# A graph layer with routed experts: longer VectorE instructions in the edge sort, and four places for finished output tiles

## The reference

```python
def reference(x, src, dst, edge_weight, ...):      # x: 12500 x 256; 212500 edges, sorted by their second list
    # graph layer
    h = layernorm(x) @ W                            # 256 x 256
    msgs = h[dst] * edge_weight[:, None]            # edge_col = dst
    x = x + segment_sum(msgs, src, 12500) + bias    # edge_row = src
    # experts: E = 8, top K = 2, D = 256, H = 512
    xn = layernorm(layernorm(x)) * gamma + beta
    logits = xn @ Wr + br
    w = softmax of the two largest logits, zero for the other experts
    for e in range(8):
        y += w[:, e] * (gelu(xn @ W1[e] + b1[e]) @ W2[e] + b2[e])
    return x + y
```

## Time and profile before

| | us |
|---|---|
| median of 3 runs | 4042.66 (4030.87 to 4053.49) |
| the profiled execution | 4048.99 |
| its span, first to last instruction | 4047.2 |
| TensorE busy | 3080.1 |
| POOL busy | 2636.6 |
| VectorE busy | 2538.3 |
| ScalarE busy | 1084.7 |

### The profile page before, as it was taken

How to read it: one execution, slowest core, us unless ns; L and a number is a source line. 1 busy time by engine, 2 the same in 40 slices (tenths; PEclk the granted TensorE clock), 3 DMA queues, 4 the chain that set the end, 5 groups by cost and what they waited for, 6 DMA issues and landing times.

```text
span 4047.2 us, 74660 instructions
## 1 busy us (share of the span) xinstructions
PE 3080.1 (76%) x20376; PEld 2068.7 (51%) x20376; DVE 2538.3 (63%) x6473; ACT 1084.7 (27%) x2341; POOL 2636.6 (65%) x2487
## 2 busy tenths in 40 slices
PE   7677434322698989989899898888998989099973
PEld 4445334321355555555555555555555556088762
DVE  8699658532466666666666666666666665145553
ACT  1353110000122222222222223222222222066542
POOL 1241778887777777777777777777777776620354
PEclk9899766655799999999999999999999999599987
DMA  5331110002344443434344434334344346552453
GB/s 156 108 110 58 36 29 13 7 10 59 111 114 116 116 117 110 117 112 117 110 114 113 115 111 118 113 110 113 112 112 120 109 116 102 174 165 86 131 179 113
DMA packets 288422, 420.11 MB, mean 104 GB/s; under 512 B 89734, under 2 KB 218315, under 8 KB 288139
## 3 DMA queue, kind: packets, MB, share of 16 engines
q0 software_dynamic: 109280, 279.33, 25.1%
q1 hardware_dynamic: 112536, 72.81, 6.4%
q10 hardware_dynamic: 66324, 64.42, 4.9%
HBM read 339.36 MB, written 76.98 MB: 103 GB/s over the span
## 4 chain that ended last, share of the span: by engine, by line
PE 35%; DVE 16%; issue 10%; POOL 6%; DVEq 5%; DMA 4%; SPq 1%; ACTq 0%; ACT 0%; POOLq 0%
PE bank L1775 13%; PE bank L1705 6%; PE bank L1758 4%; POOL area L749 4%; DVE area L1296 3%; PE bank L1707 3%; PE bank L1843 3%; PE bank L1860 2%; DVEq L1311 2%; DVE area L1304 2%; POOL zs L766 1%; DMA out_dram<-area 1%; DVE rel L1293 1%; DVEq L1304 1%; DVE rq L1341 1%
## 5 line engine op out<-in xcount | busy, mean ns | idle before, releaser
L749 POOL DMA_INDIRECT area<-h_table,listed x1856 | 1862.6, 1004 | 612.3 <-issue 545.6
L1705 PE MATMUL bank<-area 128*128 x2608 | 881.0, 386 | 75.4 <-issue 38.0
L1707 PE MATMUL bank<-area 128*128 x2608 | 718.8, 276 | 0.0
L899 ACT ACTIVATE area<-bank,b_t 128x512 f32<-128x512 f32 x384 | 263.8, 687 | 1454.1 <-PE bank L1758 902.5
L1775 PE MATMUL bank<-w2h,area 128*128 128x256 f16 x3072 | 591.3, 295 | 0.0
L1304 DVE TENSOR_TENSOR area<-area,listed 128x1024 f16 x652 | 423.0, 690 | 107.6 <-DVE area L1296 91.1
L1705 PEld LDWEIGHTS bank<-area 128*128 x2608 | 257.1, 99 | 412.4 <-issue 181.9
L717 POOL DMA_INDIRECT edge_list<-area,didx x256 | 414.8, 1620 | 77.2 <-issue 77.2
L1758 PE MATMUL bank<-area,w1h 128*128 128x512 f16 x1536 | 458.8, 381 | 0.0
L1775 PE MATMUL bank<-w2l,area 128*128 128x256 f16 x1536 | 453.8, 295 | 0.0
L1429 DVE SCALAR_TENSOR_TENSOR area<-bank,wfull,area 128x256 f32<-128x256 f32 x384 | 168.3, 480 | 302.1 <-PE bank L1775 302.1
(11 more groups left out here) (289 smaller groups left out, 4977.6 us busy)
## 6 DMA issues: line engine op xcount, KB each, us to landing
area<-h_table,listed POOLq DMA_INDIRECT x1856
area<-in_x_dram SPq DMA_DIRECT2D x194, 128.0 KB, 2.2
area<-zs SPq DMA_DIRECT2D x66, 256.0 KB, 2.8
ys<-area ACTq DMA_DIRECT2D x66, 256.0 KB
out_dram<-area ACTq DMA_DIRECT2D x100, 128.0 KB, 2.7
h_table<-area SPq DMA_DIRECT2D x97, 128.0 KB, 1.7
xt<-in_x_dram ACTq DMA_DIRECT2D x97, 128.0 KB
area<-in_L_ffn_W_dram ACTq DMA_DIRECT2D x16, 512.0 KB, 3.9
```

Of the source, the lines that this page charges most:

```text
L749: pool.indirect_dma_start(out=stage[:, (k % RU) * UNIT + 2 * D * c:(k % RU) * UNIT + 2 * D * (c + 1)], out_offset=None, in_=h_table[:, :], ...
L899: nc.scalar.activation(h32[:, m, :], psH[m][:, :], ACT.Gelu, scale=1.0 / WSCALE, bias=b1_t[:, e * KH + m:e * KH + m + 1])
L1705: nc.tensor.matmul(psA[:, :], target[:, ds(at, P, 2)], stage[:, ds(rows, 2 * D)], start=False, stop=False)
L1707: last = nc.tensor.matmul(psA[:, 0:D], target[:, ds(at + TGT // 2, P, 2)], stage[:, ds(rows, D)], start=False, stop=False)
```

## The change

Four edits:

- The output places `ot` and their semaphores `s_ofin` go from two to four (`RX`), so a combine waits for the store of the tile four before, not two before.
- The first four PSUM banks become two tensors of two banks (`twin`). One `copy_predicated` takes two banks; `s_kept` counts pairs of banks, and TensorE waits by pairs.
- `field` is stored in pairs of columns, `[CH // 2, NF, 2]`, so that one VectorE product takes all four fields of a group. The two values of a column pair stay adjacent.
- In `records` the two record parts are written for the four groups of a batch at once.

```diff
-        ot = blk(fp32, 2, D)
+        ot = blk(fp32, RX, D)
-        field = sort(fp16, NF, CH)
+        field = sort(fp16, CH // 2, NF, 2)
...
-        bank = [ctx.enter_context(nc.psum_tensor(f"bank{i}", [P, 512], fp32)) for i in range(8)]
+        twin = [ctx.enter_context(nc.psum_tensor(f"twin{i}", [P, 2, 512], fp32)) for i in range(2)]
+        bank = [twin[i // 2][:, i % 2, :] for i in range(4)]
+        bank += [ctx.enter_context(nc.psum_tensor(f"bank{i}", [P, 512], fp32)) for i in range(4, 8)]
...
-            nc.gpsimd.tensor_tensor(field[:, 3, :], wgt[:, :], field[:, 2, :], ALU.subtract).then_inc(s_wfield, 1)
+            nc.gpsimd.tensor_tensor(field[:, :, 3, :], by_two(wgt), field[:, :, 2, :], ALU.subtract).then_inc(s_wfield, 1)
...
-                for k in range(NBK):
-                    dve.wait_ge(s_place, NBK * i + k + 1)
-                    nc.vector.copy_predicated(posp[:, cols[k]], maskp[:, i % 2, cols[k]],
-                                              ps_pos[k][:, 0:BC]).then_inc(s_kept, 1)
+                for w in range(2):
+                    dve.wait_ge(s_place, NBK * i + 2 * w + 2)
+                    nc.vector.copy_predicated(by_bank(posp, w), by_bank(maskp[:, i % 2, :], w),
+                                              twin[w][:, :, 0:BC]).then_inc(s_kept, 1)
...
-                for f in range(NF):
-                    two = field[:, f, c].rearrange("p (j e) -> p j e", e=2).unsqueeze(2)
-                    ins = nc.vector.tensor_tensor(
-                        rhs[:, h, :, f, :, :], eqq[:, h, :, :, :], two.to_broadcast([P, GC // 2, Q, 2]), ALU.mult)
-                ins.then_inc(s_build, 1)
+                pairs = slice(g * GC // 2, (g + 1) * GC // 2)
+                nc.vector.tensor_tensor(
+                    rhs[:, h, :, :, :, :], eqq[:, h, :, :, :].unsqueeze(2).to_broadcast([P, GC // 2, NF, Q, 2]),
+                    field[:, pairs, :, :].unsqueeze(3).to_broadcast([P, GC // 2, NF, Q, 2]),
+                    ALU.mult).then_inc(s_build, 1)
...
-                for j in range(BATCH):
-                    nc.vector.tensor_tensor(
-                        rec[:, j, :, 0:RUN].bitcast(i32), got[:, j, 0, :].rearrange("p (r k) -> p r k", r=RQ),
-                        low3[:, j, :].rearrange("p (r k) -> p r k", r=RQ), ALU.add)
+                nc.vector.tensor_tensor(
+                    rec[:, :, :, 0:RUN].bitcast(i32), got[:, :, 0, :].rearrange("p j (r k) -> p j r k", r=RQ),
+                    low3[:, :, :].rearrange("p j (r k) -> p j r k", r=RQ), ALU.add)
...
-                if j >= 2:
-                    dve.wait_ge(s_ofin[j % 2], 16 * (j // 2))
+                if j >= RX:
+                    dve.wait_ge(s_ofin[j % RX], 16 * (j // RX))
...
-                        pe.wait_ge(s_kept, NBK * (i - 1) + k + 1)
+                        pe.wait_ge(s_kept, 2 * (i - 1) + k // 2 + 1)
```

More of the change, by code:

```diff
@@ L222, in gnn_moe_layer_kernel, with by_two @@
         area = sb("area", [P, AREA // 4], fp32)
+        def by_two(a):
+            return a.rearrange("p (j e) -> p j e", e=2)
         class Carve:
@@ L493, in gnn_moe_layer_kernel @@
         s_o = sem("s_o")
-        s_ofin = [sem("s_ofin0"), sem("s_ofin1")]
+        s_ofin = [sem(f"s_ofin{i}") for i in range(RX)]
         def reached(eng, s, value, gate=True):
@@ L790, in _ @@
             nc.scalar.activation(half_h[:, :], bkt_b[:, :], ACT.Copy).then_inc(s_cast, 1)
-            nc.scalar.activation(field[:, 2, :], wgt[:, :], ACT.Copy).then_inc(s_cast, 1)
+            nc.scalar.activation(field[:, :, 2, :], by_two(wgt), ACT.Copy).then_inc(s_cast, 1)
             act.wait_ge(s_prep, 7)
-            nc.scalar.activation(field[:, 1, :], src_i[:, :], ACT.Copy).then_inc(s_cast, 1)
+            nc.scalar.activation(field[:, :, 1, :], by_two(src_i), ACT.Copy).then_inc(s_cast, 1)
             act.wait_ge(s_prep, 8)
-            nc.scalar.activation(field[:, 0, :], dst_i[:, :], ACT.Copy).then_inc(s_cast, 1)
+            nc.scalar.activation(field[:, :, 0, :], by_two(dst_i), ACT.Copy).then_inc(s_cast, 1)
             def norm(t):
@@ L982, in store_out @@
                 act.wait_ge(s_o, j + 1)
-                act.dma_start(out_rows(routed[j]), ot[:, j % 2, :]).then_inc(s_ofin[j % 2], 16)
+                act.dma_start(out_rows(routed[j]), ot[:, j % RX, :]).then_inc(s_ofin[j % RX], 16)
             turned(0)
@@ L1000, in _ @@
             act.wait_ge(s_ost, 16 * (NSET + 1))
-            for k in range(2):
-                act.wait_ge(s_ofin[k], 16 * len(range(k, NR, 2)))
+            for k in range(RX):
+                act.wait_ge(s_ofin[k], 16 * len(range(k, NR, RX)))
         @block.vector
@@ L1119, in pair_masks @@
                     dve.wait_ge(s_place, NBK * (i - 1))
-                    dve.wait_ge(s_kept, NBK * (i - 1))
+                    dve.wait_ge(s_kept, 2 * (i - 1))
                 if i == 0:
@@ L1135, in tab, with by_bank @@
                 dve.wait_ge(s_tab, tabs[0])
+            def by_bank(a, w):
+                return a[:, 2 * w * BC:2 * (w + 1) * BC].rearrange("p (k c) -> p k c", k=2)
             cols = [slice(k * BC, (k + 1) * BC) for k in range(NBK)]
@@ L1218, in _ @@
                     places()
-            dve.wait_ge(s_kept, NBK * (NT // 2))
+            dve.wait_ge(s_kept, 2 * (NT // 2))
             nc.vector.tensor_scalar(sh_f[:, :], bucket_h[:, :], 12.0, None, ALU.mult)
@@ L1271, in records @@
                 post(nc.vector.tensor_scalar(low3[:, :, :], bint[:, :, :], 7, None, ALU.bitwise_and))
[L1272 to L1279 removed]
+                nc.vector.tensor_tensor(
+                    rec[:, :, :, 0:RUN].bitcast(i32), got[:, :, 0, :].rearrange("p j (r k) -> p j r k", r=RQ),
+                    low3[:, :, :].rearrange("p j (r k) -> p j r k", r=RQ), ALU.add)
+                nc.vector.tensor_tensor(
+                    rec[:, :, :, RUN:2 * RUN], rown[:, :, :].rearrange("p j (r k) -> p j r k", r=RQ),
+                    dest[:, :, :, 2].unsqueeze(3).to_broadcast([P, BATCH, RQ, RUN]), ALU.add).then_inc(s_posted, 1)
             for g in range(NGRP):
@@ L1677, in _ @@
                     pe.wait_ge(s_tables, 1)
-                    pe.wait_ge(s_kept, NBK * (NT // 2))
+                    pe.wait_ge(s_kept, 2 * (NT // 2))
                 if j == 0 and B >= 2:
```

8 lines of the change are left out of this document (2 added, 6 removed).

## The result

The changed kernel takes 4013.05 us at the median of 6 runs (4006.43 to 4019.76) against 4043.48 of the kernel before (6 runs, the three from before the change among them). The ratio is 0.9921, 95% interval 0.9907 to 0.9936: 30 us faster, where 3993 was forecast, inside the range of 3970 to 4022. The profiled execution took 4012.82 us (span 4010.7), 36.5 us less in the span than that of before.

A forecast was written before the change was run, and what follows sets the result against it. Limits taken: VectorE in the place loop, POOL in the sort, output-store waits in the tail. 32 + (10 + 1.2 + 0.4) + 6 = 50 us off 4048.99 gave 3999, or 3993 us for the median; range 3970 to 4022.

The forecast's parts named there:

- The tail's waits for stores: Expert blocks that also combine tiles: four places remove the combine's wait for store landing; 17 blocks, 32 us less (23 to 41).
- POOL becomes the limit or nearly: Tail: with the store waits gone, POOL's two tile fetches per block, 6.2 to 7.3 us, set or nearly set the pace.
- the 6.7 us: Tail: block pace taken for 15 of the 17 blocks, from POOL's two fetches; the first two blocks at 6.4 us.
- Products: Sort: one product of 3328 elements saves 0.20 us per group; 10 us through scatters plus 1.2 us before the first.
- The argument by held scatters: Sort: POOL gets through once per group; a held scatter's 3.30 us wait shrinks by 0.20, 6% of 167 us, 10 us.
- Records: Sort: two record instructions for eight save 0.4 us per batch; only the first batch counts, 0.4 us (0 to 6).
- Copies: Place loop: two-bank copies take 1.99 us instead of 2.12 per iteration; 48 iterations, 6 us less (0 to 17).
- The estimate of 0.25 us per iteration: Place loop: the skill's 120 cycles plus one per element for a PSUM source; two copies fewer save 12 us in all.
- The halved rate: Rival, 0.05: the sort's long product loses its doubled rate and scatters wait longer; 49 us slower, 4092 us.
- The gathers did not take the stores' place: Rival, 0.13: in the tail VectorE holds POOL's gathers, a block takes 8 us; 27 us gained in all, 4015 us.
- nor did TensorE's pace come: Rival, 0.14: the tail runs at TensorE's pace and the copies save twice as much; 65 us gained, 3978 us.
- The signs: Marks of being right: tail pace 6.4 to 6.9 us, product 1.9, long scatters 4.1, place iteration 3.6, second tail part unchanged.

## Why the prediction was right and where not

- **The tail's waits for stores.** Right in the mechanism: the landing is gone from the chain. The term was mis-sized, 32 us forecast and 15.7 measured (17 to 22 with the places alone). The step that failed is "two stores in each such block, 0.99 us together ..., which I let cost 0.25 us of the block". That issue lies in a ring through ScalarE and VectorE in which nothing is idle, so it costs all of its 1.05 us, and the read of the expert's number behind it takes 0.59 us in place of 0.28. The pace is 6.15 + 1.05 + 0.31 and 0.1 between them, 7.6 us; a block of 6.4 us was never near. I had taken 6.14 us as TensorE's pace with slack on ScalarE. The rows for the right sum stood in the trace of before, where the same stretch was 2.48 us. Why the read takes longer behind the stores stays open.
- **"POOL becomes the limit or nearly."** Wrong for this change, where POOL waited for combines 11 times, up to 1.7 us; right once the ring was shortened, at 6.33 us, which is two fetches at the quick end of my 6.2 to 7.3. That fetch time came true, and the 6.7 us did not matter.
- **Products.** Rate as forecast (1.88 us). The gain passed through POOL: 9 to 13 us alone where 11.2 were forecast. The argument by held scatters gave nearly the right size, but the runs show a simpler path: the scatters that end beside VectorE's work are fixed in number, so the whole saving, 4 x 0.2 us per batch, comes off.
- **Records.** 0.4 us forecast, 4 to 7 measured alone; my upper end was 6. That the other fifteen batches "lie inside POOL's time" was the wrong picture.
- **Copies.** 6 us forecast, and the place loop is 6.3 us shorter, but only 2 of it are the copies': 0.07 us per iteration, not 0.13. A copy of 832 elements takes 1.079 us, so 416 elements more cost 0.467 us where I had taken 0.44; of the step of 0.50 us between copies that leaves about 0.03 us as what a second copy costs for itself, and not 0.06. The estimate of 0.25 us per iteration, from the Trainium skill, VectorE: DVE Perf Modes, section on the TRN2 errata, is further off. The rest is POOL's meetings with VectorE, which the forecast did not have: the size of this term came out right by luck.
- **The rivals.** The halved rate did not come (1.88 us against the 2.8 from which it decides). Its price has a slip: 3.57 less 2.10 us is 1.47 and not 1.55, by which the same sum gives 45 us slower and not 49. The gathers did not take the stores' place in the changed kernel (no combine of the 17 blocks waits for them), though the measured 4013 us lies beside the 4015 of that rival; nor did TensorE's pace come. ScalarE's came, which I had priced and then hidden.
- **The signs.** The product of 1.88 us, the long scatters of 4.06 and the second part of the tail came as named. The block pace of 6.4 to 6.9 us did not, nor TensorE or POOL before the combine, and the place iteration is 3.67 us, not 3.6.
- **The total.** 50 us forecast, 36.5 in the profiles and 30 in the medians: 16 too much in the tail, 6 too little in the sort and just ahead of it, nearly 3 lost in stages that I had left alone, and 6 in the place loop of which 4 came by another way than the one forecast. The errors in tail and sort partly cancel, and so the forecast is nearer than its largest term. The rest of the distance to 3993 us is that the profile of before was 5.5 us slower than the median and that of the changed kernel was not.

## What to carry to other kernels

Before an issue or a register load is costed at nothing on an engine that "waits for TensorE", follow one period around through all engines: when the engine's next work stands behind that issue in its own program, the wait shown is what the ring leaves and not slack. When a buffer is released late, look first at who issues the release and behind what; here moving the stores to an idle queue was worth more than twice the places. And where POOL's transfers stand beside long two-input VectorE instructions, count the breaks between these, not their lengths.

## What the runs showed of the hardware

- POOL's indirect scatters end 0.9 us after a break in a row of VectorE's instructions with two SBUF inputs (the break is the comparison, or 0.11 us of clearing). One ends per break; in between they are 4.1 us long with one break per group and 2.0 with two, and unheld they take 0.97. Whether it is the second input that holds them no run varies.
- It goes the other way as well: a mask of 1664 elements took 2.52 us in place of 0.58 behind a POOL subtraction of 2.13. Kernels with the same code in that stage of 211 us differ by 4 to 5 us by how often they meet.
- Two copies of 832 elements out of two PSUM banks each take 2.06 us, and four of 416 take 2.12.
- ScalarE's read of a register takes 0.28 us, and 0.59 on average (up to 0.76) where it stands behind two store issues; these take 0.48 us each, and once 1.29 and once 1.85.
